# Convolution by DFT: forward transform over sums and differences of mirrored samples, norms of later chunks on ScalarE, low weight parts in another order

## The reference

```python
x = L0_attn_a_u
x = x + _L0_attn_a_ref(_layernorm(x, axis=-1), ...)      # the convolution
x = x + _L0_ffn_ref(_layernorm(x, axis=-1), ...)         # the experts

def _L0_attn_a_ref(u, A_log, D, C_re, C_im, log_dt):
    K = jnp.einsum('mn,mln->ml', C_re, jnp.exp(at))      # the taps, at from log_dt and A_log
    u_f = jnp.fft.rfft(u.transpose(0, 2, 1), n=2 * L_)
    k_f = jnp.fft.rfft(K, n=2 * L_)
    y = jnp.fft.irfft(u_f * k_f, n=2 * L_)[..., :L_]
    return y.transpose(0, 2, 1) + u * D
```

## Time and profile before

| | us |
|---|---|
| median of 3 runs (lowest to highest) | 845.89 (845.77 to 846.59) |
| the profiled execution | 846.15 |
| its span, first to last instruction | 844.1 |
| share of the span: TensorE / VectorE / ScalarE / GpSimd | 95% / 79% / 83% / 66% |
| mean granted TensorE clock | 0.994 of full speed |
| first expert matmul begins, from the span's start | 84.36 |

### The profile page before, as it was taken

How to read it: one execution, slowest core, us unless ns; L and a number is a source line. 1 busy time by engine, 2 the same in 40 slices (tenths; PEclk the granted TensorE clock), 3 DMA queues, 4 the chain that set the end, 5 groups by cost and what they waited for, 6 DMA issues and landing times.

```text
span 844.1 us, 20346 instructions
## 1 busy us (share of the span) xinstructions
PE 797.9 (95%) x7721; PEld 441.4 (52%) x7721; DVE 669.6 (79%) x1944; ACT 698.9 (83%) x864; POOL 553.6 (66%) x622
## 2 busy tenths in 40 slices
PE   6999898899999899999999999999999999999995
PEld 6444575566677533333333333333333777777774
DVE  5896899999997576777777777777645999888884
ACT  3500887788988899999999999999998899999984
POOL 2575655455543688888898899888887554545442
PEclk9999999999999999999999999999999999999998
DMA  9101000000004523333433443443410000000000
GB/s 289 42 25 51 26 2 2 1 2 2 1 2 101 101 70 94 93 93 94 98 83 86 100 101 101 101 98 79 102 25 1 3 14 14 15 14 14 14 14 16
DMA packets 37945, 46.08 MB, mean 55 GB/s; under 512 B 6121, under 2 KB 23794, under 8 KB 37842
## 3 DMA queue, kind: packets, MB, share of 16 engines
q1 hardware_dynamic: 37842, 44.73, 20.8%
HBM read 27.93 MB, written 16.78 MB: 53 GB/s over the span
## 4 chain that ended last, share of the span: by engine, by line
PE 63%; DVE 13%; ACT 12%; issue 8%; POOL 3%; DMA 0%; ACTq 0%
PE psum L837 16%; PE psum L783 15%; PE psum L1135 12%; ACT prob L1093 11%; PE psum L1084 5%; PE psum L1193 4%; DVE mixed L849 3%; DVE normed L358 3%; POOL prob L1108 3%; PE psum L587 2%; PE psum L487 2%; PE psum L552 2%; PE psum L977 1%; PE psum L658 1%; DVE hidden_parts_first L806 1%
## 5 line engine op out<-in xcount | busy, mean ns | idle before, releaser
L1093 ACT ACTIVATE prob<-psum 128x1536 f32<-128x1536 f32 x256 | 347.7, 1495 | 16.1 <-PE psum L1084 16.1
L1135 PE MATMUL psum<-prob,vstack 128*32 128x256 f32 (+1 forms) x2048 | 206.3, 498 | 1.6 <-DVE o_tok L1143 1.6
L783 PE MATMUL psum<-xt_parts,w_parts 128*128 128x512 f16 x768 | 186.6, 379 | 0.0
L849 DVE SCALAR_TENSOR_TENSOR mixed<-psum,comb_y,mixed 128x128 f32<-128x128 f32 x512 | 143.3, 341 | 2.1 <-PE psum L837 2.1
L813 POOL TENSOR_TENSOR hidden_parts_second<-hidden_second,hidden_parts_second 128x512 f16<-128x512 f32 x64 | 79.0, 1236 | 91.7 <-ACT hidden_parts_second L799 91.7
L813 POOL TENSOR_TENSOR hidden_parts_first<-hidden_first,hidden_parts_first 128x512 f16<-128x512 f32 x64 | 77.9, 1223 | 77.8 <-ACT hidden_parts_first L799 77.6
L797 ACT ACTIVATE hidden_first<-psum,b 128x512 f32<-128x512 f32 x128 | 88.5, 691 | 29.0 <-PE psum L783 22.0
L1103 POOL TENSOR_SCALAR_AFFINE_SELECT prob<-prob 128x512 f32<-128x512 f32 x128 | 82.7, 646 | 41.0 <-ACT prob L1093 35.7
L1084 PE MATMUL psum<-qstack,kstack 32*128 32x512 f16 x768 | 99.8, 385 | 9.1 <-POOL prob L1108 4.4
L1084 PEld LDWEIGHTS psum<-qstack,kstack 32*128 32x128 f16 x768 | 24.8, 91 | 158.2 <-ACT prob L1093 138.7
L837 PE MATMUL psum<-w_parts,hidden_parts_first 128*128 128x128 f16 x1536 | 96.0, 219 | 10.6 <-DVE mixed L849 5.6
(11 more groups left out here) (122 smaller groups left out, 1055.2 us busy)
## 6 DMA issues: line engine op xcount, KB each, us to landing
qstack<-qk_parts SPq DMA_DIRECT2D x128, 128.0 KB, 3.6
qk_parts<-parts SPq DMA_DIRECT2D x64, 192.0 KB, 3.2
kstack<-qk_parts SPq DMA_DIRECT2D x128, 32.0 KB, 3.5
stream<-L_attn_a_u SPq DMA_DIRECT2D x4, 512.0 KB, 7.6
kept_x<-stream SPq DMA_DIRECT2D x4, 512.0 KB, 2.7
out<-mixed SPq DMA_DIRECT2D x8, 256.0 KB, 2.3
w_whole<-L_ffn_W SPq DMA_DIRECT2D x1, 1024.0 KB, 10.8
taps<-c_taps SPq DMA_DIRECT2D x1, 640.0 KB, 6.0
```

The costliest lines, as they stand in the source:

```text
L783: last = e.matmul(bank(u % 4), m.w1[:, w_part, ex, cols], xt_parts[:, s, x_part, :], start=(n == 0), stop=(n == len(PRODUCTS) - 1))
L849: last = e.scalar_tensor_tensor(out=m.y[:, t0 + t, :], in0=bank(down_bank(m, i))[:, t * P:(t + 1) * P], scalar=comb_y[:, s, t, ex:ex + 1], ...
L1093: e.activation(prob[:, n % PROBS, :], psum[:, TILE * (n % 2):TILE * (n % 2 + 1)], ACT.Exp, scale=SCALE)\
L1135: last = e.matmul(to[SLOT * lane:SLOT * (lane + 1)], vstack[:, b % 2, keys, first:first + SLOT], weights_of(n - t, lane, keys, pair), star ...
```

## The change

Each sequence is folded. The second half of the samples is loaded a second time in reversed order (`mirror`; the host writes the reversed copy), so that row p holds sample 255-p. The norm is taken from `stream` for the first half and from `mirror` for the second. Then the sum and the difference of the two halves are formed (`folded`). With the phase of the transform put to the middle of the sequence, the cosine rows need only the sums and the sine rows only the differences, over 128 rows instead of 256. The forward matrix shrinks to half (512 to 256 KB), and each forward output becomes one matmul instead of two. The inverse keeps its shape.

The norm of chunk 0 stays on VectorE, which also does both folds of that chunk. For chunks 1 to 3 ScalarE writes the normed tiles from a scale and an offset (GpSimd makes the offset in two further small instructions), GpSimd folds the sums, and VectorE the differences.

The load of the first expert weights moves ahead of the second chunk of the stream, and ScalarE cuts them before it waits for the taps. The low parts are taken array by array: the first expert weights ahead of combine(0), the second beside the chunks, the q, k and v part in chunk 1 of the first experts, with a wait for it on TensorE before chunk 2. The waits for low parts in VectorE's, ScalarE's and TensorE's first experts now count the shares of the two expert arrays (LOWS = 8); GpSimd gets the same wait.

```diff
@@ dft_constants @@
-    sin_packed = sin.copy()
-    sin_packed[0] = nyq
-    forward = np.concatenate([cos, sin_packed])
...
+    ang = 2.0 * np.pi * np.outer(f, n - (SEQ - 1) / 2) / FREQ
+    cos, sin = np.cos(ang), -np.sin(ang)
+    sin_packed = sin.copy()
+    sin_packed[0] = nyq
+    forward = np.ascontiguousarray(np.concatenate([cos, sin_packed])[:, :P].T).astype(np.float32)
...
@@ norms of the convolution @@
+    def conv_source(t):
+        return mirror[:, t // HALVES, :] if t % HALVES else stream[:, t, :]
+
     def vector_conv_stats(e, ch):
-        e.wait_ge(s_x[ch], 16)
-        vector_norm_stats(e, conv_norm, ch, stream, ch * CONV_TILES, CONV_TILES)
-
-    def vector_conv_normed(e, ch):
-        vector_norm_out(e, conv_norm, ch, stream, ch * CONV_TILES, CONV_TILES)
+        tiles = range(ch * CONV_TILES, (ch + 1) * CONV_TILES)
+        e.wait_ge(s_x[ch], 2 * 16)
+        for t in tiles:
+            last = e.bn_stats(stats[:, t, :], conv_source(t))
...
     def gpsimd_conv_rstd(e, ch):
         gpsimd_norm_rstd(e, conv_norm, ch, ch * CONV_TILES, CONV_TILES)
+        if ch:
+            tiles = slice(ch * CONV_TILES, (ch + 1) * CONV_TILES)
+            e.tensor_scalar(neg_mean[:, tiles], meanvar[:, tiles, 0], -1.0, None, ALU.mult).then_inc(mean_negated, 1)
+            e.wait_ge(mean_negated, ch)
+            e.wait_ge(conv_norm.rstd, ch + 1)
+            e.tensor_tensor(offset[:, tiles], neg_mean[:, tiles], rstd[:, tiles], ALU.mult).then_inc(offset_ready, 1)
+
+    def vector_conv_first(e):
+        e.wait_ge(conv_norm.rstd, 1)
+        for t in range(CONV_TILES):
+            last = e.tensor_scalar(normed[:, t, :], conv_source(t), meanvar[:, t, 0:1], rstd[:, t:t + 1], ALU.subtract,
+                                   ALU.mult)
+        last.then_inc(conv_norm.out, 1)
+        e.wait_ge(conv_norm.out, 1)
+        for n, op in enumerate((ALU.add, ALU.subtract)):
+            fold(e, 0, n, op).then_inc(fold_first, 1)
+
+    def scalar_conv_normed(e, ch):
+        e.wait_ge(offset_ready, ch)
+        for t in range(ch * CONV_TILES, (ch + 1) * CONV_TILES):
+            last = e.activation(normed[:, t, :], conv_source(t), ACT.Identity, scale=rstd[:, t:t + 1],
+                                bias=offset[:, t:t + 1])
+        last.then_inc(conv_normed, 1)
+
+    def fold(e, ch, n, op):
+        halves = normed[:, ch * CONV_TILES:(ch + 1) * CONV_TILES, :].rearrange("p (b h) m -> p h b m", h=HALVES)
+        return e.tensor_tensor(folded[:, ch % 2, n, :].rearrange("p (b m) -> p b m", m=D), halves[:, 0], halves[:, 1], op)
+
+    def wait_to_fold(e, ch):
+        e.wait_ge(conv_normed, ch)
+        if ch >= 2:
+            e.wait_ge(transformed, 4 * (ch - 1))
+
+    def gpsimd_fold(e, ch):
+        wait_to_fold(e, ch)
+        fold(e, ch, 0, ALU.add).then_inc(summed_up, 1)
+
+    def vector_fold(e, ch):
+        wait_to_fold(e, ch)
+        fold(e, ch, 1, ALU.subtract).then_inc(differed, 1)
@@ sync_loads @@
             e.dma_start(stream[:, tiles, :], x_tiles[:, tiles, :]).then_inc(s_x[i], 16)
+            batches = slice(i * CONV_BATCHES, (i + 1) * CONV_BATCHES)
+            e.dma_start(mirror[:, batches, :], dr["u_mirror"][:, batches, :]).then_inc(s_x[i], 16)
...
+        e.dma_start(w1_whole[:], w1_rows).then_inc(s_w1, 16)
+        load_x(1)
         e.dma_start(skip_d[:], dr["L0_attn_a_D"].rearrange("(a n) -> a n", a=1)).then_inc(s_small, 16)
-        load_x(1)
...
         load_x(2)
-        e.dma_start(w1_whole[:], w1_rows).then_inc(s_w1, 16)
@@ scalar_taps, after the last piece of the powers @@
+        scalar_cut(e, 0, w1_flat, w1_flat, s_w1, 16)
         e.wait_ge(tapped, 1)
@@ vector_taps @@
-        vector_conv_normed(e, 0)
+        vector_conv_first(e)
@@ instead of scalar_cut_weights @@
+    def scalar_conv(e):
+        scalar_conv_normed(e, 1)
+        scalar_conv_normed(e, 2)
+        scalar_cut(e, 1, w2_flat, w2_flat, s_w2, 16)
+        scalar_cut(e, 2, qkv_flat, wqkv[:], s_attw, ATTW)
+        scalar_conv_normed(e, 3)
@@ tensor_forward @@
         if pos == 0:
             e.wait_ge(s_forward, 16)
-            e.wait_ge(conv_norm.out, ch + 1)
+        if pos < 2 and ch:
+            e.wait_ge((summed_up, differed)[pos], ch)
+        elif pos < 2:
+            e.wait_ge(fold_first, pos + 1)
...
-        for h in range(HALVES):
-            last = e.matmul(bank(pos), forward[:, h, i * P:(i + 1) * P], un[:, h], start=(h == 0),
-                            stop=(h == HALVES - 1))
-        last.then_inc(transformed, 1)
+        e.matmul(bank(pos), forward[:, i * P:(i + 1) * P], folded[:, ch % 2, i // 2, :], start=True, stop=True)\
+         .then_inc(transformed, 1)
@@ vector_conv @@
-        vector_conv_normed(e, 1)
         vector_conv_stats(e, 2)
+        vector_fold(e, 1)
...
-                vector_conv_normed(e, ch + 2)
+                vector_fold(e, ch + 2)
@@ gpsimd_conv @@
         gpsimd_conv_rstd(e, 0)
+        gpsimd_low_weights(e, 0, 0)
+        gpsimd_low_weights(e, 0, 1)
         gpsimd_conv_rstd(e, 1)
+        gpsimd_low_weights(e, 0, 2)
+        gpsimd_fold(e, 1)
         gpsimd_conv_rstd(e, 2)
+        gpsimd_low_weights(e, 0, 3)
         for ch in range(CONV_CHUNKS):
             gpsimd_combine(e, ch)
-            gpsimd_low_weights(e, ch)
+            if ch + 2 < CONV_CHUNKS:
+                gpsimd_fold(e, ch + 2)
+            gpsimd_low_weights(e, 1, ch)
@@ tensor_first @@
         for ch in range(FFN_CHUNKS):
+            if ch == 2:
+                e.wait_ge(qkv_low, CONV_CHUNKS)
             for ex in range(EXPERTS):
@@ gpsimd_first, at the end of the inner loop @@
+                if ch == 1 and ex >= EXPERTS - CONV_CHUNKS:
+                    gpsimd_low_weights(e, 2, ex - (EXPERTS - CONV_CHUNKS))
@@ kernel @@
+    arrays["u_mirror"] = np.ascontiguousarray(np.asarray(inputs["L0_attn_a_u"])[:, :P - 1:-1].transpose(1, 0, 2))
```

More of the change, by code:

```diff
@@ L105, in dft_constants @@
     inv = np.ascontiguousarray(inverse.reshape(4, P, SEQ).transpose(1, 0, 2)).astype(np.float32)
-    return by_sample(forward), by_sample(taps), inv
+    return forward, by_sample(taps), inv
 def shape_constants():
@@ L183, in build_in @@
         skip_d = sb("skip_d", [1, D], of=own)
-        forward = sb("forward", [P, HALVES, 4 * P], of=own)
+        mirror = sb("mirror", [P, BATCH, D], of=own)
+        offset, neg_mean = sb("offset", [P, TILES], of=own), sb("neg_mean", [P, TILES], of=own)
+        folded = sb("folded", [P, 2, 2, BANK], of=own)
+        forward = sb("forward", [P, 4 * P], of=own)
         taps = sb("taps", [P, HALVES, 5 * P], of=own)
@@ L283, in build_in @@
     ktap_moved, skip_added = sem("ktap_moved"), sem("skip_added")
-    scaled, high_cut, low_cut = (sem(n) for n in ("weights_scaled", "high_cut", "low_cut"))
+    scaled, high_cut, low_cut, qkv_low = (sem(n) for n in ("weights_scaled", "high_cut", "low_cut", "qkv_low_cut"))
+    LOWS = 2 * CONV_CHUNKS
     b2_high, b2_cut = sem("b2_high_cut"), sem("b2_cut")
@@ L363, in vector_norm_out @@
         vector_norm_tiles(e, norm, i, x, t0, n).then_inc(norm.out, 1)
+    def conv_source(t):
+        return mirror[:, t // HALVES, :] if t % HALVES else stream[:, t, :]
     def vector_conv_stats(e, ch):
-        e.wait_ge(s_x[ch], 16)
-        vector_norm_stats(e, conv_norm, ch, stream, ch * CONV_TILES, CONV_TILES)
-    def vector_conv_normed(e, ch):
-        vector_norm_out(e, conv_norm, ch, stream, ch * CONV_TILES, CONV_TILES)
+        tiles = range(ch * CONV_TILES, (ch + 1) * CONV_TILES)
+        e.wait_ge(s_x[ch], 2 * 16)
+        for t in tiles:
+            last = e.bn_stats(stats[:, t, :], conv_source(t))
+        last.then_inc(conv_norm.stats, 1)
+        e.wait_ge(conv_norm.stats, ch + 1)
+        for t in tiles:
+            last = e.bn_aggr(meanvar[:, t, :], stats[:, t, :])
+        last.then_inc(conv_norm.agg, 1)
@@ L507, in build_in, with scalar_cut @@
             for flat, cut in ((w1_flat, w1), (w2_flat, w2), (qkv_flat, wqkv_parts))]
[L509 to L515, removed]
-        e.mul(qkv_flat, wqkv[:], WSCALE).then_inc(scaled, 1)
-        e.wait_ge(scaled, 3)
-        e.copy(CUTS[2][1][0], qkv_flat).then_inc(high_cut, 1)
+    def scalar_cut(e, i, whole, source, landed, count):
+        e.wait_ge(landed, count)
+        e.mul(whole, source, WSCALE).then_inc(scaled, 1)
+        e.wait_ge(scaled, i + 1)
+        e.copy(CUTS[i][1][0], whole).then_inc(high_cut, 1)
+    def scalar_conv(e):
[4 more added lines that the diff above has]
+        scalar_conv_normed(e, 3)
         e.wait_ge(s_expw, EXPW)
@@ L528, in vector_cut_biases, with gpsimd_low_weights @@
                                op0=ALU.mult, op1=ALU.subtract).then_inc(b2_cut, 1)
-    def gpsimd_low_weights(e, n):
-        for i, (flat, (high, low)) in enumerate(CUTS):
-            share = flat.shape[1] // CONV_CHUNKS
-            cols = slice(n * share, (n + 1) * share)
-            e.wait_ge(high_cut, i + 1)
```

(13 more changed lines are left out.)

8 lines of the change are left out of this document (5 added, 3 removed).

## The result

| | us |
|---|---|
| before, median of 5 runs | 845.77 (844.60 to 846.59) |
| changed, median of 5 runs | 841.91 (841.37 to 843.33) |
| ratio changed to before | 0.9958 (0.9944 to 0.9973) |
| forecast | 837.3 (835.8 to 841.3) |

What follows compares the result with a forecast made beforehand. TensorE was taken to bound the convolution, VectorE and GpSimd just behind. From 846.15 us, 8.9 off (0.55 + 6.9 + 1.4) plus 0.3 gave 837.55, less 0.26 for the median 837.3; range 835.8 to 841.3.

Steps and rivals of the forecast that it cites:

- The halved blocks of chunks 2 and 3: Convolution, TensorE: each forward block goes from 6.87 to 3.44 us, 6.9 us off the path for two chunks.
- The gap ahead of inverse(1): Convolution, TensorE: the wait for VectorE's residual of chunk 0 disappears, 1.4 us off.
- Loads and the early cut: Front: mirrored loads and ScalarE's cut of the first expert weights stay hidden; cost 0, bound 0.5 us.
- The q, k, v wait's direct price: First experts, chunk 2: TensorE waits for the low parts, mostly covered by VectorE's lag; 0.3 us (0 to 3.2).
- the start of inverse(0): Convolution: the chain through khat, norm, folds and combine(0) lets inverse(0) start at 39.6, 0.55 us earlier than before.
- ScalarE's norm: Chunk 1 in the convolution: 8 tiles at 0.22 us from 27.55, 1.8 us (1.2 to 2.5), done at 29.4.
- the collision: Folds of chunk 1: VectorE's takes 0.6 us and up to 1.24 more if GpSimd holds it off; GpSimd's stays 1.24.
- the clock's price in the sum: Convolution, TensorE: clock falls around forward(1) cost 0 in the sum; 1.6 to 3.2 us if inverse(0) is struck.
- the first gap: TensorE idle from about 29 to 32.7, ahead of forward(1); a clock fall expected there, costing 0 in the sum.
- The second gap: TensorE idle from about 37 to 39.6, ahead of inverse(0); a clock fall there would cost 1.6 to 3.2 us.
- rival A: Front of the convolution: slower norms, fold collisions, clock fall in the second gap; 838.8 to 841.5 us, chance 0.20.
- Rival B: First experts: the q, k, v wait costs 3.2 us instead of 0.3 if VectorE isn't late; 840.2 us, chance 0.07.

Runs made afterwards that it cites:

- run 6: The changed kernel with every forward matmul of chunks 1 to 3 issued twice: 847.27 us, ratio 1.0016 to the kernel before.
- the first profile: Profiled execution of the changed kernel in the main measurement, the slowest of its five: 843.33 us.
- the second profile: Profile of another execution of the unaltered changed kernel, run again beside the follow-ups: 841.70 us; the median of that repeat was 841.91.
- run 2: The changed kernel with GpSimd's deviation and offset of chunk 2 ahead of its fold of chunk 1: 837.61 us.
- run 4: The changed kernel with TensorE's q, k, v wait ahead of chunk 6 of the first experts instead of chunk 2: 840.34 us.
- run 1: The changed kernel plus eight unused matmuls, four in TensorE's gap behind forward(0) and four in the gap ahead of inverse(0): 839.72 us.
- run 8: The changed kernel with low shares early, deviation of chunk 2 before fold of chunk 1, chunk 1's norm on VectorE, q, k, v wait at chunk 6: 833.34 us.
- run 11: The kernel of run 8 with the norm of chunk 1 on ScalarE again: 837.17 us.
- run 3: The changed kernel with the norm of chunk 1 on VectorE and without GpSimd's offset for that chunk: 840.38 us.
- run 9: The changed kernel with the norms of all chunks on VectorE, without ScalarE's norms and GpSimd's offsets: 843.40 us.
- run 10: The kernel of run 8 with TensorE's q, k, v wait back at chunk 2: 834.36 us.
- run 12: The kernel of run 8 with the norms of all chunks on VectorE: 840.11 us.

## Why the prediction was wrong

**Right.** The halved blocks of chunks 2 and 3, 6.9 us, by the profile (each took 3.43 where it had taken 6.87) and by run 6. The gap ahead of inverse(1), 1.4 us, is gone. Loads and the early cut are free: the last exponential ends at 13.4, ScalarE cuts from 13.34 to 17.17, long before the taps. The q, k, v wait's direct price: TensorE waits 2.65 us at 131.20 and is 0.26 us late a chunk later.

**Wrong: the start of inverse(0), "39.6".** This is the step that failed; it was 43.00 and 41.98. The links of the chain, in the first profile:

- The norm of chunk 1 began 1.1 us late (28.64 for 27.55), behind khat. L561 took 3.2 us and not the 2.2 of the kernel before. I had tied the slow slots to the first four matmuls at 21.4; in the runs the clock rises anywhere from 24.6 to 27.5 us with the same work ahead, and in the second profile this link is only 0.1 late. (The subtraction printed in the prediction, 5.19 less four times 0.85, isn't 3.4; the 3.4 that it goes on with is four slots of 0.85.)
- ScalarE's norm took 3.1 to 3.2 us for 1.8, beyond my upper bound of 2.5, which came from shapes without a scale and a bias per partition.
- GpSimd's fold took 0.5 more and combine(0) 0.5 more, in which it gave way to VectorE, while I had charged the collision to VectorE alone.

They add up to 3.4 because every link was serial, and to 2.4 in the second profile. The order made them serial: GpSimd's 2.6 us for chunk 2 stood behind a fold that waits for ScalarE. The forecast had these 2.6 us in its chain, so they don't explain the miss; but I called them a term instead of looking at what the order cost, and run 2 shows it to be the largest single loss of the change, 4.3 us with the clock.

**Wrong: the clock's price in the sum, 0.** I expected a fall in the first gap, absorbed by forward(1), and that came. The second gap was to be 2.6 us and got no price in the sum. It was 3.42 in the first profile, 2.18 in the second and 2.14 in run 4, and each time the clock was low under inverse(0) and cost 1.8 us. So the late start doesn't explain this term: a gap shorter than the forecast one had the fall too, and the 0 had no row behind it. The price is inside the 1.6 to 3.2 that I had named for it, and run 1 shows it as a cost of its own. The Trainium skill, TensorE: Matmul & The Clock Gate, section "HAM oscillation — how this bites in real kernels", describes this pattern of short bursts with gaps between. The runs agree in that the clock fell at both gaps, 4.4 and 2.1 to 3.4 us, around a forward(1) of four matmuls. In run 6, with forward(1) doubled and no second gap, it fell only at the first.

**Wrong: the q, k, v wait's whole price, "0.3".** It is 0.3 without and 1.9 with a fall of the clock. I had applied the clock to the convolution only.

Of the signs of being wrong that the prediction names, two came: a granted clock below 1 after 39.6, and a norm on ScalarE of over 2.5 us. Of its cases rival A came true, for which it had 838.8 to 841.5: a late start and the clock in the second gap. Rival B, the wait in full for want of VectorE's lag, did not come; the fall of the clock at the wait was in none of the cases. From the second profile: start 2.4, clock under inverse(0) 1.8, clock at the wait 1.6, together 5.8 of lost gain against the 4.6 by which the forecast was off. Of the difference of 1.2, 0.84 lies in the attention: from its first exponential to the transposes of chunk 1 of the second experts it took 374.03 us in the profile before, 375.39 and 373.19 in the two of the changed kernel, 373.19 in run 8 and 375.10 in run 11, always with the same code. The granted clock is below full in some profiles between 280 and 296 us, in others not. What decides this wasn't tried, and single profiles can't be compared to better than 2 us for that reason.

## What to carry to other kernels

When work is taken off the bounding engine, trace the chain that starts it, not only the steady state: here the later chunks gained as forecast, and the start lost 4 to 5 us of the 8.9, in its chain and in the clock. On an engine that is idle for another (GpSimd here, 3.2 us), put everything whose inputs are ready ahead of the instruction that waits; a swap of two lines (run 2, 4.3 us) was worth more than a norm moved to another engine (run 3, 1.5 us). And after a reduction of TensorE's work look at each of its gaps, in every later stage too: a wait that another engine's lag covers may still cost the clock.

## What the runs showed of the hardware

- ScalarE's instruction with a scale and a bias per partition, 128x128 in float32 from SBUF to SBUF, takes 0.48 us and 0.385 from start to start; the copy of 128x128 from PSUM takes 0.27 (the second khat copy at 28.49).
- TensorE's clock fell to 0.50 ahead of forward(1) in all seven profiles with 4.4 us of idling there, and in the four with 2.7 to 3.5 us (runs 3, 9, 10, 12); it stayed up in run 8 (1.75) and in run 1 (gap filled, 0.93 left). Ahead of inverse(0), behind such a fall, it was low again after 2.14, 2.18, 3.02 and 3.42 us and stayed up after 0.65 to 0.77. After 3.45 us ahead of inverse(1) it fell in run 12 (8.64 us to the next start) and after 3.47 us in run 9 it didn't (6.94). Behind two gaps of 1.26 and 2.65 us with 1.5 us of work between, it fell in five of nine profiles. It doesn't fall at the same place in each execution of the same kernel.
- VectorE's fold and GpSimd's instruction on SBUF delay each other both ways: GpSimd's 128x512 took 1.72 to 1.78 us instead of 1.27 where a fold of VectorE started just ahead of it, and VectorE's fold took 0.86 to 1.78 instead of 0.69 where it started beside a running instruction of GpSimd. Before, GpSimd's 1.28 had not moved while VectorE's norm went from 2.14 to 5.94.
